# Last stage of a ViT block on one core: part of the gather before the last stores, and the last block-diagonals spread over three engines

## What is computed

```python
dist = softmax(mean(x @ Wr + br, axis=1))          # one distribution over 16 heads per image
_, idx = top_k(dist, 4)
idx = sort(idx)                                    # slot s of an image holds its s-th chosen head
Qs, Ks, Vs = (gather(Q), gather(K), gather(V))     # only the chosen heads, 64 features each
score = softmax(einsum('bhqd,bhkd->bhqk', Qs, Ks) * scale)
O = einsum('bhqk,bhkd->bhqd', score, Vs)           # 128 images x 4 slots x 17 tokens x 64
O = O.transpose(0, 2, 1, 3).reshape(b, s, 4 * 64)
return O @ Wo + bo                                 # added to h
```

## Time and profile before

| | before |
|---|---|
| median of 3 runs | 384.56 us |
| lowest, highest | 382.87, 386.45 us |
| the profiled execution | 382.7 us |
| its span in the profile | 380.9 us |
| mean granted TensorE clock | 0.852 |
| busy TensorE / VectorE / ScalarE / GpSimd | 313.3 / 253.1 / 206.0 / 170.8 us |

### The profile page before, as it was taken

The page is one execution under the profiler, slowest core; times in us unless marked ns, Lnnn a source line. Parts: engine busy times, 40 slices in busy tenths (PEclk is TensorE's granted clock), DMA queues, the critical chain, the costliest instruction groups (busy, mean ns, idle before and its releaser), DMA issues.

```text
span 380.9 us, 14271 instructions
## 1 busy us (share of the span) xinstructions
PE 313.3 (82%) x5994; PEld 253.1 (66%) x5994; DVE 253.1 (66%) x549; ACT 206.0 (54%) x468; POOL 170.8 (45%) x199
## 2 busy tenths in 40 slices
PE   0999999977978687875699556998999997965786
PEld 0797777634666465654588354988988996953366
DVE  2355456565478888888498467677887897582365
ACT  1013333274896666662278532796887976550420
POOL 4656000002446666662135252586666778583200
PEclk9999999999985555555599756999999999897989
DMA  6998810001800000000000048688999899712614
GB/s 203 372 422 278 275 59 0 0 0 43 290 4 3 4 5 4 5 3 3 4 0 2 1 148 273 191 259 284 276 312 276 263 300 307 221 29 58 228 58 179
DMA packets 43916, 53.77 MB, mean 141 GB/s; under 512 B 16940, under 2 KB 40652, under 8 KB 43340
## 3 DMA queue, kind: packets, MB, share of 16 engines
q1 hardware_dynamic: 37380, 49.16, 39.1%
q10 hardware_dynamic: 5896, 1.48, 1.8%
q0 software_dynamic: 576, 2.23, 1.7%
HBM read 45.04 MB, written 7.81 MB: 139 GB/s over the span
## 4 chain that ended last, share of the span: by engine, by line
PE 36%; SPq 19%; DVE 17%; issue 10%; DMA 6%; ACT 6%; POOL 5%; POOLq 0%; ACTq 0%; DVEq 0%
SPq L510 16%; PE ps L1440 10%; PE ps L1463 5%; PE ps L1594 4%; DVE r L1103 4%; POOL r L583 4%; PE ps L1803 3%; DVE rs L1113 2%; DMA r<-in_x 2%; DVE mx L1088 2%; PE ps L1643 2%; PE ps L1478 2%; PE ps L1523 2%; SPq L442 2%; DMA ring<-wsplit 2%
## 5 line engine op out<-in xcount | busy, mean ns | idle before, releaser
L576 POOL TENSOR_TENSOR r<-r,cst 128x1088 f32<-128x1088 f32 x16 | 32.9, 2061 | 61.6 <-DVE ring L1039 58.7
L1440 PE MATMUL ps<-r 128*128 128x256 f32 x192 | 45.7, 393 | 8.9 <-DMA r<-in_x 8.9
L1440 PEld LDWEIGHTS ps<-r 128*128 128x128 f32 x192 | 37.4, 198 | 16.1 <-issue 10.5
L870 ACT ACTIVATE r<-ps 128x448 f16<-128x448 f32 x55 | 34.8, 659 | 21.9 <-PE ps L1643 21.2
L1545 PE MATMUL ps<-r 17*32 17x34 f32 x2048 | 30.4, 242 | 16.1 <-DVE r L1103 11.5
L1545 PEld LDWEIGHTS ps<-r 17*32 17x32 f32 x2048 | 27.2, 142 | 24.1 <-DVE r L1103 18.6
L798 ACT ACTIVATE r<-r,cst 128x136 f32<-128x136 f32 x128 | 39.9, 400 | 0.0
L671 POOL TENSOR_TENSOR r<-r,quad 128x476 f16<-128x476 f16 x38 | 37.3, 1004 | 0.6
L1670 PEld LDWEIGHTS ps<-r,ring 128*128 128x128 f16 x840 | 31.7, 101 | 5.7 <-DMA ring<-wsplit 3.0
L1670 PE MATMUL ps<-r,ring 128*128 128x68 f16 x840 | 32.8, 201 | 3.1 <-DMA ring<-wsplit 2.6
L583 POOL TENSOR_TENSOR r<-r,rinv 128x544 f32<-128x544 f32 x16 | 18.2, 1140 | 35.7 <-DVE rinv L1117 35.7
(11 more groups left out here) (172 smaller groups left out, 698.8 us busy)
## 6 DMA issues: line engine op xcount, KB each, us to landing
ring<-wsplit SPq DMA_DIRECT2D x140, 192.0 KB, 3.3
r<-in_x SPq DMA_DIRECT2D x3, 1536.0 KB, 16.0
r<-in_w SPq DMA_DIRECT2D x4, 768.0 KB, 7.1
wsplit<-ring SPq DMA_DIRECT2D x1, 3072.0 KB, 11.7
r<-in_x SPq DMA_DIRECT2D x4, 384.0 KB, 9.2
h<-in_pos SPq DMA_DIRECT2D x1, 1536.0 KB, 12.2
out<-h SPq DMA_DIRECT2D x3, 512.0 KB, 2.7
pair_rows<-r ACTq DMA_DIRECT2D x6, 224.0 KB
```

The source lines that it names most:

```text
L870: nc.scalar.activation(dst, src, ACT.Copy).then_inc(fill_act, 1)
L1440: mm = pe.matmul(bank((n - 1) % 2, 0, D), xT[:, c, k, i * P:(i + 1) * P], tokw[:, k, :], start=k == 0, stop=k == PKT - 1)
```

## The change

Six edits, all in the part after the routing:

1. `gather_early(s)` for slots 0, 2 and 1: as soon as the stores of the first 6 units (7 for slot 1) have landed, GpSimd gathers those rows whose pair lies in them; the bound of the DMA skips the others. It stands between the block-diagonals of unit 8 and the split of unit 9.
2. VectorE makes `idx_late` at v = 0: pairs below the bound get 4096 added, so that the gather behind the stores skips them. The late gathers go in the order 0, 1, 3, 2; slot 3 is gathered only there.
3. The users of a slot that is gathered twice wait for 32 instead of 16.
4. The block-diagonals of `weigh2(8, 1)` go from GpSimd to ScalarE, in eight pieces, four before the exponent of unit 9 and four behind it.
5. One block-diagonal of `weigh2(9, 0)` goes from GpSimd to VectorE, ahead of `head_out(8, 1)`.
6. `keep_awake(24)` behind the stores becomes `keep_awake(12)`.

```diff
+        EARLY = {0: NV - 4, 2: NV - 4, 1: NV - 3}
+        LATE_ORDER = (0, 1, 3, 2)
+        NOWHERE = 4096
...
+            def gather_early(s):
+
+                for i in range(2):
+                    pool.wait_ge(o2_stored[i], 32 * len(range(i, EARLY[s], 2)))
+                pool.wait_ge(idx_ready, 2)
+                rows = PU * EARLY[s]
+                pool.indirect_dma_start(og[:, s, :], None, pair_rows[0:rows],
+                                        bass.IndirectOffsetOnAxis(ap=idx[:, s:s + 1], axis=0),
+                                        bounds_check=rows - 1, oob_is_err=False)                    .then_inc(og_ready[s], 16)
...
-            for r in range(2):
-                for x in range(2):
-                    block_diagonal(NV - 2, r, x)
+            for x in range(2):
+                block_diagonal(NV - 2, 0, x)
+            for s in EARLY:
+                gather_early(s)
             split_high(NV - 1)
             split_low(NV - 1)
-            for x in range(2):
-                block_diagonal(NV - 1, 0, x)
+            block_diagonal(NV - 1, 0, 0)
             for n in range(biased(NV - 1), NTOK):
                 add_bias(n)
+            for s in EARLY:
+                pool.wait_ge(og_ready[s], 16)
             for i in range(2):
                 pool.wait_ge(o2_stored[i], stores(i))
-            pool.wait_ge(idx_ready, 1)
-            for s in range(NSLOT):
-                pool.indirect_dma_start(og[:, s, :], None, pair_rows,
-                                        bass.IndirectOffsetOnAxis(ap=idx[:, s:s + 1], axis=0))\
-                    .then_inc(og_ready[s], 16)
+            for s in LATE_ORDER:
+                if s in EARLY:
+                    pool.indirect_dma_start(og[:, s, :], None, pair_rows,
+                                            bass.IndirectOffsetOnAxis(ap=idx_late[:, s:s + 1], axis=0),
+                                            bounds_check=NPAIR - 1, oob_is_err=False).then_inc(og_ready[s], 16)
+                else:
+                    pool.indirect_dma_start(og[:, s, :], None, pair_rows,
+                                            bass.IndirectOffsetOnAxis(ap=idx[:, s:s + 1], axis=0))\
+                        .then_inc(og_ready[s], 16)
...
             pick(NV - 1)
+            block_diagonal(NV - 2, 0)
             exponent(NV - 1)
+            block_diagonal(NV - 2, 1)
             v_out(NV - 1, 1)
...
+                for s in EARLY:
+                    dve.tensor_scalar(aside[:, s:s + 1], at_slot[:, s:s + 1], float(PU * EARLY[s]), float(NOWHERE),
+                                      ALU.is_lt, ALU.mult).then_inc(set_aside, 1)
+                dve.wait_ge(set_aside, len(EARLY))
+                dve.tensor_tensor(idx_late[:, 0:len(EARLY)], at_slot[:, 0:len(EARLY)], aside[:, 0:len(EARLY)], ALU.add)\
+                    .then_inc(idx_ready, 1)
...
             v_low(NV - 1, 1)
+            dve.wait_ge(pT_low, NV)
+            dve.wait_ge(pv2_done, 2 * (NV - 3) + 1)
+            dve.tensor_tensor(free(bd_of(NV - 1)[:, 1, 0, :], (TCOL, GR), (NTOK, IPG), (1, NTOK)),
+                              free(p2Tx[:, (NV - 1) % 2, 1, 0], (QROW, GR), (0, IPG), (1, NTOK)),
+                              free(quad[:, :], (0, GR), (1, IPG), (0, NTOK)), ALU.mult).then_inc(bd_ready, 1)
             head_out(NV - 2, 1)
...
-                if last:
-                    pe.wait_ge(bd_last, 2 * IPG)
+                if r == 1 and v >= NV - 2:
+                    pe.wait_ge(bd_last, 2 * IPG * (v - NV + 3))
...
-            keep_awake(24)
+            keep_awake(12)
```

More of the change, by code:

```diff
@@ L198, in build @@
         idx = sb("idx", NSLOT, I32)
+        idx_late = sb("idx_late", NSLOT, I32)
+        aside = sb("aside", NSLOT)
         heads = sb("heads", WORDS * NV, I32)
@@ L296, in build @@
         idx_ready = sem("idx_ready")
+        set_aside = sem("set_aside")
         hbo_ready = sem("hbo_ready")
@@ L332, in build, with gathered_rows @@
         stored = sem("stored")
+        def gathered_rows(s):
+            return 32 if s in EARLY else 16
         def turned_pairs(c):
@@ L957, in _, with block_diagonal @@
             v_out(NV - 1, 0)
+            def block_diagonal(v, x):
+                act.wait_ge(pT_low if x else pT_high, v + 1)
+                act.wait_ge(pv2_done, 2 * (v - 1))
+                for i in range(IPG):
+                    nc.scalar.activation(free(bd_of(v)[:, x, GR, NTOK * i:], (TCOL, GR), (1, NTOK)),
+                                         free(p2Tx[:, v % 2, x, GR], (QROW, GR), (1, NTOK)), ACT.Copy,
+                                         scale=quad[:, i:i + 1]).then_inc(bd_last, 1)
             pick(NV - 1)
+            block_diagonal(NV - 2, 0)
             exponent(NV - 1)
+            block_diagonal(NV - 2, 1)
             v_out(NV - 1, 1)
             for x in range(2):
[L962 to L968, removed]
+                block_diagonal(NV - 1, x)
             act.wait_ge(ld["late"], LATE)
@@ L978, in _ @@
                 s = 2 * k + 1
-                act.wait_ge(og_ready[s], 16)
+                act.wait_ge(og_ready[s], gathered_rows(s))
                 for lo, hi in ((0, OG_FIRST), (OG_FIRST, NTOK)):
@@ L1352, in _, with late_rows @@
             one_hot(2 * PU, 4 * PU)
+            def late_rows():
+                for s in EARLY:
[4 more added lines that the diff above has]
+                    .then_inc(idx_ready, 1)
             for v in range(NV - 1):
@@ L1356, in _ @@
                     one_hot(4 * PU, NPAIR)
+                    late_rows()
                 if v >= 1:
@@ L1400, in lay_out @@
             def lay_out(s):
-                dve.wait_ge(og_ready[s], 16)
+                dve.wait_ge(og_ready[s], gathered_rows(s))
                 for lo, hi in ((0, OG_FIRST), (OG_FIRST, NTOK)):
@@ L1707, in weigh2 @@
                 last = (v, r) == (NV - 1, 1)
-                if last:
-                    pe.wait_ge(bd_last, 2 * IPG)
+                if r == 1 and v >= NV - 2:
+                    pe.wait_ge(bd_last, 2 * IPG * (v - NV + 3))
                 else:
-                    pe.wait_ge(bd_ready, 4 * v + 2 * r + 2)
+                    pe.wait_ge(bd_ready, 4 * v + 2 * r + 2 - 2 * (v == NV - 1))
                 if v < 2:
```

## The result

| | before | after |
|---|---|---|
| median of 20 runs each | 383.46 us | 385.03 us |
| lowest, highest | 379.22, 386.52 us | 381.86, 388.24 us |
| the profiled execution | 382.7 us | 384.9 us |
| its span in the profile | 380.9 us | 383.1 us |
| mean granted TensorE clock | 0.852 | 0.849 |

What follows compares the result with a forecast made beforehand. One dependent line through the last stage bounds the kernel, its late gathers bound by transfer. 0.25 lost ahead and 2.57 gained behind the stores give -2.3 us: 382.7 becomes 380.4, median 382.3, range 379.6 to 385.5.

Steps and rivals of the forecast that it cites:

- up to the last store I charged 0.25 us: Ahead of the last store: early gathers take 3.64 us on GpSimd, other moved work mostly fits idle time; loss 0.25 us.
- the sign of being wrong that the prediction had set at 1 us: At the last store: the forecast is wrong if that store goes out over 1 us later.
- F: Before unit 9's split: early gathers hold it, needing 2.3 us beyond 3.64; 384.6 us and more, chance 0.04.
- Rival G: Last stores: unit 9's stores queue behind the early gathers' data, costing about 1 us; 383.3 us, chance 0.06.
- The clock: At the output matmuls: the first 24 run at half clock as before; twelve dummies last until 354.8, no cost charged.
- Rival D: At the output matmuls: the shorter stretch keeps 2.4 GHz, saving 1.84 us more; 380.4 us, chance 0.14.
- Rival E: Behind the stores: dummies end before the clock rises, turning and output matmuls run slow; up to 389.3 us, chance 0.09.
- VectorE's block-diagonal: Ahead of head_out(8,1): the block-diagonal moved to VectorE takes 0.65 us, bounds nothing and 0.98; unit 8's store at 343.8.
- Behind the stores: Late gathers: 194 rows move instead of 512; slots 0 and 1 ready at 352.9 and 354.2; gain 2.57 us.
- rival C: Late gathers: skipped rows cost as much as moved ones, nothing gained, 0.25 lost; 384.8 us, chance 0.08.
- rival B: Late gathers: VectorE's copy of slot 0 holds up GpSimd's issue by 1.27 us; 383.6 us, chance 0.09.
- The mis-sized term: Late gathers: slot 2 ready at 358.2, between 357.3 and 359.5, its copy starting there instead of 360.77; gain 2.57 us.

Runs made afterwards that it cites:

- early_two: Changed kernel with early gathers of slots 0 and 1 only, late order 0, 1, 2, 3, and 24 dummies; 381.85 us, ratio 0.998 to the original.
- spread_only: Original kernel plus only the moved block-diagonals (edits 4 and 5), no early gathers, 24 dummies; 381.39 us, ratio 1.004 to the original.
- before_again: The original kernel run again unchanged, as control; 382.15 us, ratio 0.995 to the original on the same chip.
- two_again: Repeat of early_two, the same kernel with two early gathers and 24 dummies; 382.24 us, ratio 0.997 to the original.
- after_again: The changed kernel run again unchanged, three early gathers and 12 dummies; 386.90 us, ratio 1.002 to the original.
- dummies24: The changed kernel with 24 dummies instead of 12, three early gathers kept; 382.92 us, ratio 1.003 to the original.
- gathers_behind: Changed kernel with the three early gathers moved behind the last weigh2, while the last stores land, and 24 dummies; 388.01 us, ratio 1.018 to the original.

## Why the prediction was wrong, point by point

- **The step that failed: up to the last store I charged 0.25 us.** Most of its parts held: GpSimd 3.79 us for the gathers, no wait for the stores of units 0 to 6, ScalarE's eight pieces in idle time. It priced an early gather as GpSimd's time alone; what it left out is that an indirect gather holds TensorE, whose signals came 0.92 and 1.40 us late. A grew by 0.8 to 1.6 us in after, the sign of being wrong that the prediction had set at 1 us. I had taken the price of an issue from rows in which TensorE ran dummies, whose ends nobody waits for the earlier trace rows; there such a hold has no reader. Of the rivals F and G named the early gathers as a loss ahead of the stores' landing, by other paths (the split held; unit 9's stores queued behind their data); the split started 0.12 us after its input.
- **The clock: the second failed step.** The forecast had the first 24 output matmuls at half clock as in the earlier trace rows, so that fewer dummies cost nothing, and "the clock back at 1.00 before the turning" as the test. It was back, at 357.5, and fell again before the output matmuls. Against the 4.46 us of the profile before, they took 5.30; against the 2.79 that they take with 24 dummies and an equally short C, edit 6 cost 2.5 us, and 2.9 with the turning between them. Rival D's gain was there to be had (D is 3.07 with 24 dummies in six profiles), and the twelve dummies gave it away. Rival E had the place right and asked for the dummies to end before the clock rises, which they did not.
- **VectorE's block-diagonal** took 1.14 us here, 0.65 was taken, 0.98 was the upper bound. It took 1.12 to 1.15 us in the seven profiles in which GpSimd's block-diagonal or bias addition ran beside most of it, and 0.64 or 0.65 in the four in which GpSimd was done or nearly (0.80 in early_two). In five of the seven, and in early_two, GpSimd's addition of 0.72 us took 1.13 or 1.14. So 0.65 was right for VectorE alone, and the sum left out what the two cost each other. It was behind the late signals by then, and spread_only, in which it took 1.13, shows no cost of it in A.
- **Behind the stores the mechanism was right.** Slots 0 and 1 were used 2.89 and 4.18 us behind the first dummy (forecast 3.5 and 5). Skipped rows cost nearly nothing, so rival C fell: an empty late gather is in use 2.18 us after its issue began (353.29 to 355.47). VectorE's copy of slot 0 ran from 355.47 to 356.69 beside slot 3's issue, which took 0.97 us from 355.95: rival B fell. By the rule of the Trainium skill in "SBUF — State Buffer", section "SBUF: two separate sides", that issue should have been held until the copy's end; this trace does not show it. The page ties its rule to a copy in a two-port mode; whether this one ran in it, no run shows: its two parts, 256 and 832 elements a partition, took 0.29 and 1.01 us.
- **The mis-sized term behind them** is slot 2: 9.2 us behind the first dummy, not 8.6. Its issue began at 357.23 and the data landed 4.54 us later, at 188 GB/s in that stretch rather than 278. From the copy to the output matmuls it was 3.27, as forecast 3.26. The gain in C was 1.4 to 2.0 rather than 2.57: against the 14.46 of the profile before, and against the 13.85 of before_again.
- **Rival G** named the wrong store. Unit 9's went out clear of the early data. Unit 7's second piece, issued at 341.67, took 6.54 us to land among it, and head_out(9,0), which overwrites its source, waited for that: 1.24 us of idle time, 0.24 of it beyond weigh2(9,0)'s end at 348.07.
- **The balance:** A +0.8 to 1.6, B -0.0 to -0.6, C -1.4 to -2.0 and D +1.2 to 2.9 give anything from -0.6 to +3.1 us. The 20 runs say +1.6 by the medians and +2.3 by the ratio. That the time still fell into the stated range, 379.6 to 385.5, and within 1% of before, is luck: a gain of nearly the forecast size met two losses that the sum did not have, and the change went the other way.

## What to carry to other kernels

Price a moved software gather by what the other engines have to signal while it is issued, not by its own duration on GpSimd; rows in which they run filler don't show that. Where the early part of a transfer is worth a little, one or two early issues kept clear of a group of matmuls that somebody waits for gave as much here as three. Shorten a row of dummies only after looking at the clock in the stretch where it is needed, since a shorter stage can need as many as before.

## What was not expected of the hardware

- While GpSimd issues indirect gathers, with or without rows to move, TensorE is held or its signals come late: 0.52 us with one issue, 0.92 and 1.40 in after, 1.90 in two_again, 2.97 in after_again and 3.06 in dummies24. Plain DMAs of the same size, issued by GpSimd or SP, do not do this. By which path they meet is not settled: the trace shows no wait on TensorE and no shared resource. During the late gathers nothing of it is seen: in after, after_again and gathers_behind one signal of turned heads each falls due 0.7 to 0.9 us into a late issue (in after at 358.09), and it comes in time. Why is open as well.
- Placing the gathers in GpSimd's idle time before the last key copy, where TensorE waits for weights anyway, was not tried.
- An indirect gather with every row skipped still takes GpSimd 1.0 to 1.2 us.
